# Cross-attention on one Trainium2 core: the weights-times-values product taken every second step for four tiles, both value tiles of a step in one PSUM bank with one copy, and two banks for the key pieces

## The reference, cut to what matters

```python
q = proj(layernorm(x), Wq, bq)         # 32 x 16 heads x 56 x 16
k = proj(ctx, Wk, bk)                  # 32 x 16 heads x 1500 x 16
v = proj(ctx, Wv, bv)
scores = clip(q @ k.T / 4, -50, 50)    # masked columns at -10000, clipped too
probs = softmax(scores); probs = probs / (probs.sum(-1) + 1e-8)
delta = (probs @ v) @ Wo.T + bo        # scaled, layer norm, affine, added to x
```

## Time and profile before

| | us |
|---|---|
| median of 3 runs | 1723.23 |
| lowest, highest | 1722.34, 1724.77 |
| profiled execution, its own time | 1722.45 |
| its span in the trace | 1720.7 |
| PE busy | 1568.1 |
| PE weight loads busy | 1320.2 |
| DVE busy | 1420.9 |
| ACT busy | 1119.0 |
| POOL busy | 756.5 |
| mean granted share of PE's clock | 0.953 |

### The profile page before, as it was taken

One profiled execution on the slowest core, in us unless ns is written; L12 is line 12 of the kernel. 1 busy time (PEld: TensorE's weight loads), 2 busy tenths in 40 slices (PEclk: granted clock), 3 DMA queues, 4 the chain that ended last, 5 costly groups with the idle time before them and its releaser, 6 DMA issues. The chain is left out here.

```text
span 1720.7 us, 45808 instructions
## 1 busy us (share of the span) xinstructions
PE 1568.1 (91%) x18290; PEld 1320.2 (77%) x18290; DVE 1420.9 (83%) x2513; ACT 1119.0 (65%) x2155; POOL 756.5 (44%) x743
## 2 busy tenths in 40 slices
PE   5899999998747999999999999999999999999464
PEld 5888888887426888888888888888888888888233
DVE  3788778777385889889889899899899898898698
ACT  3566565565345777777777777777777777777463
POOL 1566555555154334434435434544444344342133
PEclk9999999999777999999999999999999999999667
DMA  6000000000041111111111111111111111110001
GB/s 191 2 1 2 2 2 0 2 0 1 0 146 49 50 50 50 47 41 50 50 50 50 50 49 50 40 47 50 50 50 50 50 50 49 39 50 2 1 14 30
DMA packets 41614, 66.70 MB, mean 39 GB/s; under 512 B 7749, under 2 KB 40194, under 8 KB 41282
## 3 DMA queue, kind: packets, MB, share of 16 engines
q1 hardware_dynamic: 41410, 63.93, 12.8%
HBM read 62.08 MB, written 1.84 MB: 37 GB/s over the span
## 5 line engine op out<-in xcount | busy, mean ns | idle before, releaser
L1146 POOL TENSOR_TENSOR xa_CW<-xa_CTX,xa_CH 128x500 fp32r<-128x500 f32 x187 | 307.6, 1645 | 590.5 <-ACT xa_CH L1340 590.5
L1368 DVE TENSOR_TENSOR xl_ACC<-xl_ACC,xl_PB 125x896 f32<-125x896 f32 x320 | 437.9, 1368 | 11.0
L1332 ACT ACTIVATE xl_PB<-banks,xl_BIB,xl_SCB 125x896 f32<-125x896 f32 x384 | 401.4, 1096 | 32.0 <-PE banks L1204 31.6
L1359 DVE TENSOR_SCALAR xl_PB<-xl_PB 125x896 f32<-125x896 f32 x384 | 250.5, 652 | 63.9 <-ACT xl_PB L1332 62.8
L1314 ACT ACTIVATE xl_V<-banks 125x256 f32<-125x256 f32 x384 | 147.9, 385 | 154.7 <-PE banks L1171 154.7
L1171 PE MATMUL banks<-xa_WVhigh,xa_CH 128*125 128x256 f32 x768 | 238.7, 311 | 0.0
L1171 PE MATMUL banks<-xa_WVlow,xa_CH 128*125 128x256 f32 x768 | 216.0, 281 | 0.0
L1171 PE MATMUL banks<-xa_WVhigh,xa_CW 128*125 128x256 f32 x768 | 215.9, 281 | 0.0
L1305 ACT ACTIVATE xl_KXhigh<-banks,xa_bk 128x500 fp32r<-128x500 f32 x192 | 130.5, 680 | 100.3 <-PE banks L1171 100.3
L1220 PE MATMUL banks<-xl_PB,xl_V 125*32 125x112 f32 x6144 | 187.2, 262 | 1.5 <-DVE xl_PB L1359 1.5
L1375 DVE SCALAR_TENSOR_TENSOR xl_KXlow<-banks,xa_bk,xl_KXhigh 128x500 fp32r<-128x500 f32 x192 | 137.5, 716 | 54.9 <-ACT xl_KXhigh L1305 54.3
(11 more groups left out here) (235 smaller groups left out, 3972.2 us busy)
## 6 DMA issues: line engine op xcount, KB each, us to landing
xa_CTX<-in_ctxT SPq DMA_DIRECT2D x93, 500.0 KB, 3.6
fw_WO<-in_W_o SPq DMA_DIRECT2D x1, 2048.0 KB, 17.6
xq_WR<-in_w_gating SPq DMA_DIRECT2D x1, 2048.0 KB, 9.0
X<-in_x SPq DMA_DIRECT2D x1, 1792.0 KB, 9.9
out<-ff_R SPq DMA_DIRECT2D x16, 112.0 KB, 1.9
fw_QUT<-in_W_quT SPq DMA_DIRECT2D x1, 1536.0 KB, 12.2
xa_CTX<-in_ctxT SPq DMA_DIRECT2D x1, 1500.0 KB, 14.2
xq_WL<-in_w_linear SPq DMA_DIRECT2D x1, 1024.0 KB, 11.1
```

The source lines that it names most:

```text
L1146: nc.gpsimd.tensor_tensor(context_piece(CW, i), context_piece(CTX, i), context_piece(CH, i), ALU.subtract).then_inc(ctx_low, 1)
L1332: nc.scalar.activation(PB[t % PR][:, :, :], banks[0:TK, 2 * i:2 * i + KT, 0:QW], ACT.Exp, scale=SCB[j][:, t:t + 1], bias=BIB[j][:, t:t + 1 ...
L1359: nc.vector.tensor_scalar(pt, pt, E_HI, E_LO, ALU.min, ALU.max).then_inc(clipped, 1)
L1368: nc.vector.tensor_tensor(ACC[j][:, :, :], prev[:, :, :], PB[t % PR][:, :, :], ALU.add).then_inc(summed, 1)
```

## The change

Four things change in the order of `cross_loop`, and the work itself stays: no matmul is added or removed.

- `values_product` runs only after the scores of even steps and takes four tiles (64 instructions in one section). The buffers for values and probabilities become six instead of four (`PR`), and V is one tensor.
- Both value tiles of a step go into one bank (4), one after the other, and ACT copies them out with one instruction of 512 columns. PE waits for that copy before the next step's values.
- Key pieces alternate between banks 5 and 7, so a piece waits for the low part of the piece two before it.
- `project` moves behind the keys of s = 3, and `read_delta` and the first steps of the layer norms move one step later.

```diff
-PR = 4
+PR = 6
...
-    V_BANK, O_BANK, K_BANK = (4, 5), 6, 7
+    V_BANK, O_BANK, K_BANK = 4, 6, (5, 7)
+    D_BANK = K_BANK[1]
...
-    PROJECT, NORM, ADD_DELTA = 3, {4: (0, 1), 5: (2,), 6: (3,), 10: (4, 5), 11: (6,)}, (6, 8, 9)
+    PROJECT, NORM, ADD_DELTA = 3, {5: (0, 1), 6: (2,), 7: (3,), 10: (4, 5), 11: (6,)}, (7, 8, 9)
...
-                def values(n, u, tiles, early=False):
-
-                    for i in tiles:
+                def values(n, u):
+
+                    if n:
+                        pe.wait_ge(v_ready, n)
+                    for i in range(2):
                         t = 2 * u + i
-                        if not early:
-                            pe.wait_ge(v_ready, n * 2 + i - 1)
...
                 def values_product(n, u):
 
-                    pe.wait_ge(v_ready, n * 2 + 2)
-                    for i in range(2):
+                    pe.wait_ge(v_ready, n + 1)
+                    for i in range(-2, 2):
                         t = 2 * u + i
                         pe.wait_ge(clipped, n * 2 + i + 1)
...
-                            if pu == 0 and not (first and j == 0):
+                            if pu == 1 and not (first and j == 0):
 
                                 pe.wait_ge(d_read, b)
-                            values_product(n - 1, pu)
+                            if pu % 2 == 1:
+                                values_product(n - 1, pu)
                             if pu == STEPS - 1:
                                 denominators(b - 1, 1 - j)
                         if more(last, s, 1):
-                            values(n + 1, (u + 1) % STEPS, (0,))
-                        if s == PROJECT and not first:
-
-                            pe.wait_ge(k_ready, n + K_AHEAD)
-                            project(g - 1)
-                        if more(last, s, 1):
-                            values(n + 1, (u + 1) % STEPS, (1,))
+                            values(n + 1, (u + 1) % STEPS)
                         if more(last, s, K_AHEAD):
 
-                            pe.wait_ge(k_ready, n + K_AHEAD)
-                            if s == PROJECT and not first:
+                            pe.wait_ge(k_ready, n + K_AHEAD - 1)
+                            if s == PROJECT + 1 and not first:
                                 pe.wait_ge(delta_ready, g)
...
                             keys(n + K_AHEAD, i)
+                        if s == PROJECT and not first:
+
+                            pe.wait_ge(k_ready, n + K_AHEAD)
+                            project(g - 1)
 
                 pe.wait_ge(ones_ready, 1)
                 for p in range(K_AHEAD):
-                    if p:
-                        pe.wait_ge(k_ready, p)
+                    if p >= 2:
+                        pe.wait_ge(k_ready, p - 1)
                     keys(p, p)
...
-                def values_out(n, u, early=False):
-
-                    if not early:
-                        act.wait_ge(pv_done, n - 1)
-                    for i in range(2):
-                        act.wait_ge(v_done, n * 2 + i + 1)
-                        nc.scalar.activation(V[(2 * u + i) % PR][:, :], bank[V_BANK[i]][0:TK, 0:H], ACT.Copy).then_inc(v_ready, 1)
+                def values_out(n, u):
+
+                    if n >= 3:
+                        act.wait_ge(pv_done, (n - 1) // 2)
+                    act.wait_ge(v_done, n + 1)
+                    t = 2 * u % PR
+                    nc.scalar.activation(V[:, t:t + 2, :], bank[V_BANK][0:TK, 0:2 * H].rearrange("t (i h) -> t i h", i=2), ACT.Copy).then_inc(v_ready, 1)
...
-                        if s == 5 and not first:
+                        if s == 6 and not first:
                             delta_rstd(g - 1)
...
-                        if s == PROJECT and not first:
+                        if s == PROJECT + 1 and not first:
                             read_delta(g - 1)
```

More of the change, by code:

```diff
@@ L1038, in cross_loop @@
         KX = [sb(f"KX{part}", [P, KT, CL], F32R) for part in ("high", "low")]
-        V = [sb(f"V{i}", [TK, H]) for i in range(PR)]
+        V = sb("V", [TK, PR, H])
         PB = [sb(f"PB{i}", [TK, KT, QW]) for i in range(PR)]
@@ L1241, in project @@
                     for kt in range(KT):
-                        mm = nc.tensor.matmul(bank[K_BANK][0:T, 0:H], CN[:, kt, :], WO[:, kt, :], start=(kt == 0), stop=(kt == KT - 1))
+                        mm = nc.tensor.matmul(bank[D_BANK][0:T, 0:H], CN[:, kt, :], WO[:, kt, :], start=(kt == 0), stop=(kt == KT - 1))
                     mm.then_inc(delta_done, 1)
@@ L1325, in pair @@
                             act.wait_ge(s_done, n * 2 + i + 1)
-                            if not (first and s < 2):
-                                act.wait_ge(pv_done, n - 1)
+                            if n >= PR // 2:
+                                act.wait_ge(pv_done, (n - 1) // 2)
                                 if t >= PR:
@@ L1334, in pair @@
                         if more(last, s, 1):
-                            values_out(n + 1, (u + 1) % STEPS, first and s == 0)
+                            values_out(n + 1, (u + 1) % STEPS)
                         if more(last, s, C_AHEAD):
@@ L1348, in _ @@
                     if p == 1:
-                        values_out(0, 0, early=True)
+                        values_out(0, 0)
                 pairs(act, pair)
@@ L1374, in keys_low @@
                     dve.wait_ge(kh_ready, p + 1)
-                    nc.vector.scalar_tensor_tensor(out=KX[1][:, m, at], in0=bank[K_BANK][:, 0:CK], scalar=bk[:, m:m + 1],
+                    nc.vector.scalar_tensor_tensor(out=KX[1][:, m, at], in0=bank[K_BANK[p % 2]][:, 0:CK], scalar=bk[:, m:m + 1],
                                                    in1=KX[0][:, m, at], op0=ALU.add, op1=ALU.subtract).then_inc(k_ready, 1)
@@ L1383, in read_output @@
                     src = by_head(0)
-                    dve.wait_ge(pv_done, b * STEPS + STEPS)
+                    dve.wait_ge(pv_done, (b * STEPS + STEPS) // 2)
                     dve.wait_ge(den_done, b + 1)
@@ L1415, in read_delta @@
                     dve.wait_ge(delta_done, g + 1)
-                    nc.vector.scalar_tensor_tensor(out=DL[:, :], in0=bank[K_BANK][0:T, 0:H], scalar=RS[:, 0:1], in1=BO[:, :],
+                    nc.vector.scalar_tensor_tensor(out=DL[:, :], in0=bank[D_BANK][0:T, 0:H], scalar=RS[:, 0:1], in1=BO[:, :],
                                                    op0=ALU.mult, op1=ALU.add).then_inc(delta_ready, 1)
```

13 lines of the change are left out of this document (7 added, 6 removed).

## The result

The kernel became slower. Its median is 1735.1 us (1732.64 to 1735.81, 4 runs) against 1723.78 us (1722.34 to 1724.77, 4 runs): 1.0072 times the time before, interval 1.0059 to 1.0084. The profiled execution took 1734.9 us, its span 1732.8.

A forecast was written before the change was run, and what follows sets the result against it. PE was taken as the bound, its sections adding up to the loop's time. Savings of 12.0 (sections), 4.3 (projection), 1.3 (start) and 0.1 (loop's end), 17.7 us, took 1723.2 to 1705.5 us, range 1702 to 1713.

The forecast's parts named there:

- Part 1: Loop's product: 192 sections of 32 become 96 of 64, each removed one saving 0.12 to 0.13 us, 12.0 us.
- rivals of the feed: Long product sections outrun PE's instruction supply: 1805 us; chance 0.07, shared with DVE as the bound.
- section's cost: Rival: scores followed by values cost as much as the removed product section, 1717.5 us; chance 0.03.
- the estimate with the Trainium skill: Long product sections: at about 62 ns per MATMUL, queue of 64, the change costs some 75 us: 1780 us.
- Part 2: Projection moved behind the keys of s = 3: a 0.29 us wait and restart goes in 15 pairs, 4.3 us.
- it is 0.3 to 0.4 us early: DVE's read of the projection in s = 4 ends that long before PE wants the keys' bank.
- Part 3: Two key banks: nothing gained in the loop, 1.3 us before it, bounds 0.8 and 1.7.
- Part 4: Joint value copy: ACT issues 192 copies for 384, gain hidden behind PE; values wait for no copy.
- What DVE does to this: Section on DVE lagging in PE's uneven steps: counted 0.5 us wait a pair at the denominators, 8 us in all.
- I take no wait: Two or three long adds shorten by up to 0.95 us, cancelling the counted denominators' wait; range keeps 0 to 0.8 a pair.
- waits take part of it: Rival: DVE late at denominators or projection read in s = 4, 0.2 to 0.8 us a pair, 1709 to 1718 us; chance 0.13.
- the 0.07 for slower: Chance given to a slower kernel, by the instruction feed or by DVE as the bound.

The follow-up runs named there:

- the half clip: The changed kernel with DVE's clip on 448 of the 896 columns: 1703.37 us, 0.9881 of the kernel before.
- the short POOL piece: The changed kernel with POOL's context subtraction on 50 of 500 columns from step 6 on: 1703.99 us, 0.989 of the kernel before.
- old places: The changed kernel with layer-norm and affine steps at their places before the change, projection read ahead of the first clip of s = 4: 1710.73 us.
- the read alone: The changed kernel with DVE's read of the projection ahead of the first clip of s = 4: 1727.31 us.
- the four-tile product alone: The kernel before with only the four-tile product every second step and six buffers, all other places as before: 1737.65 us, 1.0081.
- the moves alone: The kernel before with only layer-norm steps 0 to 3 and the first affine step one step later: 1739.64 us, 1.0095.

## Why the prediction was wrong

It said 1705.5 us, 1702 to 1713, faster with 0.89. Measured were 1735.1.

**Part 1, the sections: right.** Scores followed by values cost nothing extra, and the steps came out at 4.46, 6.13 and 6.53. In the runs without waits a pair is 65.34 us, 1.12 less than 66.46; with 0.28 of it for the projection, six sections gave 0.84, 0.14 each, against 0.125. The rivals of the feed (1805) and of the section's cost (1717.5) are refuted by the half clip and the short POOL piece alike. That includes the estimate with the Trainium skill, "TensorE: Matmul & The Clock Gate", section "Wait — 56ns, not 53.3ns?": 80 matmuls at 24 ns show no 62 ns pace here. (By its own terms that estimate comes to 63 us and not 75: 38 ns for 12 matmuls in 64 sections and for 28 in 32.)

**Part 2, the projection: right in what leaves, wrong in what comes.** Step s = 3 fell from 6.53 to 5.35 us, 0.28 more than its section. But "it is 0.3 to 0.4 us early" failed: the first clip of s = 4 begins 2.74 us after the scores, not 2.09, because DVE comes late out of s = 3. The keys wait, and s = 4 pays 0.42. The read ahead of that clip mends it.

**Part 3, two banks: mis-sized.** The start gave 4.0 us, not 1.3. I had bounded the clock's rise by the moments seen before; without the gap the clock rose much sooner (below). And "two banks give nothing there", said of the loop, was read from even steps: with uneven ones, at the old places, they are worth 6 us.

**Part 4, the joint copy: right.** PE lists no wait for ACT's copy.

**"What DVE does to this" is the step that failed.** The count itself was good: PE's five steps from s = 7 would take 25.7 us (26.84 measured, less 1.03 and 0.11 of waits), DVE's list 27.3, a wait of 0.5 at the denominators (0.59 measured). Then I argued it away with shorter adds: "I take no wait". The adds did shorten. From the first clip of s = 7 to that of s = 0 the ten of them took 15.4 us before and 13.2 after, 2.2 less, as much as I had hoped for. But DVE's list did not shrink below 27.3 us, it grew to 28.8 (1043.94 to 1072.72). Three things were wrong in the step to no wait.

- I priced POOL's holding-up on the adds alone. POOL's piece that misses an add meets what stands next to it: in the same stretch the ten clips grew by 1.1 us, the two normalizing instructions (L1409, L1412) by 1.1 and 0.55 and the copy of two columns by 1.1. With the 0.4 of the moved layer-norm step these are 4.2 us against the 2.2 won.
- I looked at POOL's piece in the long steps only. It falls behind the second add in s = 6, but ahead of it in s = 8 and s = 10, where DVE is late by then. And in the short step s = 7 it now starts 4.46 us after the scores (1046.20 against 1041.74), just before the second add at 1046.78. Before, it started at 5.1, just after (1043.40 against the add's 1043.05).
- I priced the moved layer-norm steps at 0.4 us of DVE. They also move POOL's multiplication, into the stretch in which POOL also spreads the queries. Alone that costs 16 us.

The sum with what was measured, on the profiled spans: 1720.7 − 17.5 (sections and projection; 16.3 forecast) − 4.0 (start) + 31.1 (waits, none of them in the first pair) + 2.2 and 0.3 (ahead of the first key piece and behind the last scores) = 1732.8 us. Sections and projection are read from the half-clip run, in which no pair has a wait. The rival "waits take part of it" had the mechanism and two of the places, but 0.2 to 0.8 us a pair where it was 2.15. That makes the 0.07 for slower far too small: DVE was 91 of 100 us busy and longer than PE over five steps by my own count.

The Trainium skill would have given the second point. I had used from "SBUF — State Buffer", "Who interferes with whom", only the case of two SBUF inputs. The same section says that copies and `tensor_scalar` can use both ports too and then shut GpSimd out, or are shut out, for a whole instruction. The Trainium skill's "VectorE: DVE Perf Modes", "Mode 2×_2P — use both read ports for one tensor", says that fp32 is enough for it. The trace had shown it: the clip of 896 columns takes 0.61 us and the add of 896 takes 1.09. The runs agree, with clips up to 1.71 us and a copy at 1.25.

**What stays open.** How the 24 us between the version with old places and the kernel after divide between the layer-norm places and the read is known only within some microseconds (the read alone 7.8). What moves the start of the first key piece by up to 4.5 us between profiled runs was not looked into. Part of the loss of the four-tile product alone was not separated, as said.

## What to carry to other kernels

A sum over the sections of the bound engine holds only while the next busiest engine still fits its shortest stretch, and at 91% busy that has to be counted step by step, with the neighbour on its port in it. Before moving a step of side work, look at every engine that it issues to, and at what that engine and its neighbour do at the new place. If two engines hold each other up, let the one with time to spare start second.

## What the runs showed of the hardware

- DVE and POOL shut each other out whole instructions at a time, whichever starts first: an add 1.09 or up to 2.20 us, a clip 0.61 up to 1.74, a multiplication of 112 columns 0.26 up to 1.35, and 2.05 where two POOL instructions followed each other (the moves alone, in the kernel before), a copy of 2 columns 0.16 or 1.25; a context piece on POOL 1.28 or up to 2.19.
- The granted clock rose from 0.50 (1.2 GHz) to full (2.4 GHz) sooner when PE had not stopped. After the change PE worked from 526.84 without a gap and the share was 0.87 in the window from 530 to 531 and 1.00 in the next. Before, PE worked from 524.62, stood still for 1.54 us, went on at 529.03, and the share was 0.50 until 534. It is no chance of one run: from the last matmul of key piece 0 to the first scores the four profiled kernels with the stop took 8.9 to 9.2 us, the twelve without it 4.8 to 6.3.

The windows of the kernel after:

```profile
530.00:531.00 1.00, 1.00 (x6) 0.83 (x5) 0.55 (x1) 0.42 (x1) 0.00 (x0) 0.87 0.97 374
531.00:532.00 1.00, 1.00 (x9) 0.95 (x8) 0.19 (x1) 0.59 (x1) 0.00 (x0) 1.00 0.13 48
```
